# A decoder layer on one core: row buffers turned by one slot, two weight pieces behind the first queries, and another order of VectorE's steps in the first attention turn

## What is computed

```python
x = x + s5(layernorm(x))        # scan over axis 0 (4 steps): z = Re-pair of V(A z + u), u = Vinv dt x; 2*Re(z)
x = x + xattn(layernorm(x), ctx) # 16 heads of 32, softmax over the sequence's 77 context rows, Wq Wk Wv Wo
x = x + ffn(layernorm(x))        # W_exp (512->2048), butterfly of 11 stages, gelu,
                                 # butterfly of 11 stages, W_con (2048->512), biases
return x                         # all float32
```

## Time and profile before

| | us |
|---|---|
| median of 3 runs | 2254.57 (2254.3 to 2255.26) |
| the profiled execution | 2254.27 |
| its span, first to last instruction | 2252.1 |
| stage one, up to the first scores | 253.6 |

### The profile page before, as it was taken

One profiled execution on the slowest core, in us unless ns is written; L12 is line 12 of the kernel. 1 busy time (PEld: TensorE's weight loads), 2 busy tenths in 40 slices (PEclk: granted clock), 3 DMA queues, 4 the chain that ended last, 5 costly groups with the idle time before them and its releaser, 6 DMA issues.

```text
span 2252.1 us, 41275 instructions
## 1 busy us (share of the span) xinstructions
PE 2215.3 (98%) x15960; PEld 1938.7 (86%) x15960; DVE 1701.0 (76%) x2854; ACT 1229.4 (55%) x2735; POOL 466.2 (21%) x578
## 2 busy tenths in 40 slices
PE   8999889999999999999999999999999999999999
PEld 7788678888888888789989989989989989889899
DVE  6775688888888888867957858758669678579467
ACT  3666566766666776635535436446346355355343
POOL 3530222222322223200110300300300300300203
PEclk8999899999999999999999999999999999999999
DMA  8999623323323331476686786786686776766765
GB/s 319 338 353 312 204 94 109 109 83 122 124 86 113 108 106 62 162 259 187 215 264 178 223 266 177 222 267 203 194 268 208 220 233 212 245 206 213 226 189 194
DMA packets 202091, 443.35 MB, mean 197 GB/s; under 512 B 32442, under 2 KB 70586, under 8 KB 200362
## 3 DMA queue, kind: packets, MB, share of 16 engines
q1 hardware_dynamic: 201898, 440.72, 60.5%
HBM read 341.66 MB, written 99.01 MB: 196 GB/s over the span
## 4 chain that ended last, share of the span: by engine, by line
PE 84%; DVE 6%; ACT 5%; DMA 3%; issue 1%; SPq 0%; POOL 0%; DVEq 0%; ACTq 0%; POOLq 0%
PE ps L455 68%; PE ps L2005 5%; PE ps L1973 4%; PE ps L1984 2%; ACT es L1099 2%; DMA x_scratch<-xa 2%; PE ps L1937 1%; ACT wc_h L1055 1%; PE ps L1894 1%; PE ps L1825 1%; DVE st L1292 1%; DVE rsum L1507 1%; ACT es L1104 1%; DMA x<-x_scratch 1%; DVE ql L1329 1%
## 5 line engine op out<-in xcount | busy, mean ns | idle before, releaser
L455 PE MATMUL ps<-ring,gh 128*128 128x256 f32 x3584 | 652.8, 284 | 0.1
L455 PEld LDWEIGHTS ps<-ring,gh 128*128 128x128 f32 x3584 | 558.3, 192 | 2.1 <-DVE gl L1329 1.5
L455 PE MATMUL ps<-xth,ring 128*128 128x512 f32 x1792 | 553.4, 389 | 0.6 <-ACT U L1209 0.6
L455 PE MATMUL ps<-ring,gl 128*128 128x256 f32 x1792 | 506.9, 283 | 0.0
L455 PEld LDWEIGHTS ps<-xth,ring 128*128 128x128 f32 x1792 | 336.4, 188 | 70.7 <-issue 1.0
L1197 ACT ACTIVATE gh<-G 128x512 fp32r<-128x512 f32 x384 | 239.2, 629 | 218.7 <-PE ps L455 218.3
L455 PE MATMUL ps<-xtl,ring 128*128 128x512 f32 x896 | 348.6, 389 | 0.0
L455 PEld LDWEIGHTS ps<-ring,gl 128*128 128x128 f32 x1792 | 343.5, 192 | 0.0
L1329 DVE TENSOR_TENSOR gl<-G,gh 128x512 fp32r<-128x512 f32 x384 | 276.1, 731 | 51.3 <-ACT gh L1197 50.2
L1180 ACT ACTIVATE G<-G,up_b 128x512 f32<-128x512 f32 x192 | 138.9, 723 | 222.0 <-DVE G L1625 222.0
L880 POOL TENSOR_TENSOR es<-es,rinv 128x308 f32<-128x308 f32 x256 | 180.0, 735 | 386.3 <-DVE rinv L1511 386.3
(11 more groups left out here) (234 smaller groups left out, 4379.3 us busy)
## 6 DMA issues: line engine op xcount, KB each, us to landing
ring<-wup_scratch SPq DMA_DIRECT2D x224, 512.0 KB, 3.8
ring<-wdn_scratch SPq DMA_DIRECT2D x224, 512.0 KB, 3.7
X<-x_scratch SPq DMA_DIRECT2D x32, 1024.0 KB, 8.8
xa<-in_x SPq DMA_DIRECT2D x16, 1024.0 KB, 8.8
x_scratch<-xa SPq DMA_DIRECT2D x16, 1024.0 KB, 10.8
x<-x_scratch SPq DMA_DIRECT2D x16, 1024.0 KB, 5.6
x_scratch<-x SPq DMA_DIRECT2D x16, 1024.0 KB, 4.3
out_x<-X SPq DMA_DIRECT2D x15, 1024.0 KB, 7.8
```

The lines of the kernel that those rows point to most:

```text
L455: mm = pe.matmul(bank, a, b, start=first and i == 0, stop=last and i == n - 1, skip_group_check=go_on)
```

## The change

The ring of row buffers is turned by one slot: group `g` uses `(g + 4) % 5`, so group 15 uses slot 4, and slots 0 to 3 come free one group earlier. `x1[0]`, `x1[1]` and `x1[2]` are loaded in groups 12, 13 and 14; `x1[2]`'s load after stage one goes. Slot 4 is now under `qh` (written from the second group's first query on, which gets a wait for all sixteen stores), and `wqh` goes where `qh` was; its copy waits for piece 56 instead of the store of group 11. `X` and `rawx` of the FFN move by 8 KB to match. Group 15 has three pieces; the last two, 70 and 71, go on PE behind the first four queries, on ScalarE behind the four high copies of them, on SyncE behind the store of group 15. PE's wait for all pieces moves behind scores(0) of the first turn. In that turn VectorE makes `lo_p(0, 0)` ahead of `shift(2)`, `lo_p(1, 0)` ahead of `shift(3)` and `lo_q(3)` ahead of the mixing of the first FFN weights; its waits for the stage buffers and the cleared buffer move up with `lo_p(0, 0)`.

```diff
-    wqh = r2.put("wqh", [P, KC, D], F32R)
+    qh = r2.put("qh", [P, KC, GT], F32R)
...
-    qh = r2.put("qh", [P, KC, GT], F32R)
+    wqh = r2.put("wqh", [P, KC, D], F32R)
...
-    r3 = Region(free_first)
+    r3 = Region(free_first + 4 * KC * GT)
...
-        PER_GROUP = [0, 0, 6, 6, 5, 5, 5, 5, 5, 5, 5, 5, 5, 5, 5, 5]
+        PER_GROUP = [0, 0, 6, 6, 5, 5, 5, 5, 5, 5, 5, 5, 5, 5, 5, 3]
+        LATE = range(PIECES - 2, PIECES)
-        xslot = lambda g: (g + 3) % XS
+        xslot = lambda g: (g + 4) % XS
...
-                        n = g - (NG - 3)
-                        if n in (0, 1):
+                        n = g - (NG - 4)
+                        if n in (0, 1, 2):
                             after(sp, x1_loaded, n * 16)
...
+            for n in LATE:
+                piece_out(n)
             stored(sp, x1_stored, NG - 1)
-            load_x1(2)
...
-                        act.wait_ge(x1_stored, 16 * (NG - 4))
+                        act.wait_ge(piece_pe, DL)
...
+            for n in LATE:
+                piece_back(n)
...
                     exp(2)
+                    act.wait_ge(x1_stored, 16 * NG)
                     hi_q(0)
...
                     sums(1)
-                    shift(2)
                     for i, out in enumerate(stage_out):
                         dve.wait_ge(out, stage_turns(PIECES, i))
                     dve.wait_ge(p_zero, 1)
                     lo_p(0, 0)
+                    shift(2)
                     lo_q(0)
                     spread2(2, range(0, 2))
                     lo_q(1)
                     sums(2)
+                    lo_p(1, 0)
                     shift(3)
-                    lo_p(1, 0)
                     spread2(2, range(2, T))
                     sums(3)
                     lo_q(2)
+                    lo_q(3)
                     mix_weights(0)
-                    lo_q(3)
...
             for o in range(KC):
                 query(ps[:, o, :], o).then_inc(pre_pe, 1)
+            for n in LATE:
+                piece(n)
             pe.wait_ge(x1_ready, KC * NG)
-            pe.wait_ge(piece_act, PIECES)
...
                 if g == 0:
                     scores(0)
+                    pe.wait_ge(piece_act, PIECES)
```

More of the change, by code:

```diff
@@ L243, in decoder_layer @@
     spots = []
-    for at, end in ((after_keep, after_keep + 4 * T * D), (r3.at, es_end)):
+    for at, end in ((after_keep, after_keep + 4 * T * D), (free_first, free_first + 4 * KC * GT), (r3.at, es_end)):
         while at + 4 * 2 * GT <= end:
@@ L463, in decoder_layer @@
         PIECES = 4 * MC + 8
-        PER_GROUP = [0, 0, 6, 6, 5, 5, 5, 5, 5, 5, 5, 5, 5, 5, 5, 5]
-        assert sum(PER_GROUP) == PIECES and len(PER_GROUP) == NG
+        PER_GROUP = [0, 0, 6, 6, 5, 5, 5, 5, 5, 5, 5, 5, 5, 5, 5, 3]
+        LATE = range(PIECES - 2, PIECES)
+        assert sum(PER_GROUP) + len(LATE) == PIECES and len(PER_GROUP) == NG
         VALUES_AT = (0, 2), (1, 0), (1, 2)
         stage_turns = lambda n, i: 16 * ((n - i + STAGES - 1) // STAGES)
-        xslot = lambda g: (g + 3) % XS
+        xslot = lambda g: (g + 4) % XS
         x_turns = lambda g: 16 * (g // XS + 1)
```

## The result

| | before | after |
|---|---|---|
| median of 12 runs each | 2255.07 us (2249.69 to 2257.01) | 2258.83 us (2255.39 to 2262.46) |
| the profiled execution | 2254.27 us | 2257.13 us |
| its span | 2252.1 us | 2254.9 us |

The ratio is 1.0021 [1.0013, 1.003]: slower by a hair over 0.2%, some 4.7 us; the two medians themselves lie 3.8 us apart. The forecast was 2256.7 us, and the median lies 2.1 us above it; against the kernel before it was +2.4 us, where 3.8 to 4.7 were measured.

The account below looks back on a forecast made before the run. TensorE is busy 98% of the span, so only some 11 us of idleness and 4 us of slow clock could be touched. +3.8 us at the third maxima less 1.4 gave 2254.3 + 2.4 = 2256.7 us, range 2250.3 to 2260.5.

Parts of the forecast that it names:

- the gate: First turn: GpSimd's clearing waits for the late stores, so the first transposes of probabilities start at 267.7 us, 3.8 later.
- my own signs: Prediction wrong if clearing starts before 260 us, group 12's store lands at 215.4, or 292 us's shift isn't the end's.
- The slip of group 12's store: SyncE's queue: the earlier first row load puts 1 MB ahead of this store, making it 2.6 us later; bounds 0 and 3.5.
- The transposes of the normalised rows: PE, before the first queries: they wait for ScalarE behind piece 68's copy and start at 234.6 us, against 235.07.
- neither gain nor loss: At the first scores: 0.5 us and the shorter group set against a longer stretch at half clock, taken as zero.
- rival (a): Slip absent or late stores not last; the load taken off the path gives nothing: 2254.1 us, chance 0.22.
- the late stores landing with group 15's: SyncE's stores of the two late pieces land where group 15's store landed, 260.48 plus the slip: 263.1 us.
- rival (b): Group 14's store lands 4.5 us earlier, slip small, clock holds, queries start 5 us earlier: 2249 us, chance 0.14.
- rival (c): PE idles some 4 us ahead of the first transposes of probabilities, the clock falls, +2.6 us: 2259.3 us, chance 0.20.
- VectorE's order: First turn, third maxima to next turn's first maxima: 23.04 - 2.0 + 0.6 = 21.6 us, a gain of 1.4 us.
- now run while PE makes the third scores: First turn: three low copies of 0.68 us on VectorE leave the stretch behind the third maxima, -2.0 us.
- From there on each turn follows the one before: After the next turn's maxima: the shift of +2.4 us there goes unchanged to the end.

Follow-up runs that it names:

- kernel 1: The changed kernel measured again with no edit, against the kernel before: 2259.36 us, ratio 1.0022.
- kernel 3: The changed kernel with `wqh` put between `xt2l` and `kh`, 16384 bytes from `xt2h`: 2255.52 us, ratio 1.0009 to the kernel before.
- kernel 7: The changed kernel with 128 bytes ahead of `wqh`, making its distance to `xt2h` 21504 bytes: 2258.8 us, one execution.
- kernel 8: kernel 3 with 384 bytes ahead of `wql` and all buffers behind it, distance of `wqh` to `xt2h` still 16384: 2257.35 us, one execution.
- kernel 6: kernel 3 with GpSimd's wait for the stage buffers and clearing of `pt2` moved behind the first tile's multiplications: 2252.27 us, ratio 0.9988 to the kernel before.
- kernel 10: The changed kernel, placement kept, with GpSimd's clearing moved behind the first multiplications: 2255.58 us, ratio 1.001 to the kernel before.
- kernel 11: kernel 6 measured again beside kernel 9 and kernel 10 on one chip: 2252.16 us, ratio 0.9991 to the kernel before.
- kernel 4: The kernel before with only VectorE's new order in the first attention turn: 2252.74 us, ratio 0.9992.
- kernel 2: The kernel before with only `wqh` and `qh` exchanged, FFN buffers moved by 8 KB and the copy's wait changed: 2257.35 us, ratio 1.0019.
- kernel 9: kernel 4 with GpSimd's clearing moved behind the first multiplications: 2253.49 us, ratio 0.9991 to the kernel before.

## Why the prediction was right or wrong

The time came out inside the range and near the forecast, and that is in part luck: a loss of 3.6 us that I hadn't in my sum, 14 turns of slower query matmuls, stands where the sum had the gate. By my own signs the account was wrong in two of three points for the first profile: the clearing started at 257.97 us and not after 260, and the shift of -1.20 us at 290 us wasn't the shift at the end, +2.87. In kernel 1, where the clearing came at 260.27 us, the shift still grew, from +0.47 to +4.62.

**The slip of group 12's store: right in kind, too large.** 216.94 less 215.39 is 1.55 us, not 2.6, in the first profile; the size of single landings varies as much as that.

**The transposes of the normalised rows: right in place.** 233.92 us where I had 234.6, by the smaller slip; ScalarE's copy of piece 68 (230.45 us) stands ahead of them, as worked out. But I took neither gain nor loss from there to the first scores, and the first maxima came 1.18 us earlier, no more than such shifts vary between kernels with the same code up to there. At the medians nothing is left: with the ring and without late pieces the ratio is 0.9994, and the order alone has 0.9992. The 3 us that VectorE no longer waits for the load are worth nothing measurable, as rival (a) said of this edit.

**The gate: right, with a landing put together wrongly.** I had the late stores landing with group 15's, at 263.1 us. They land 3 to 4 us behind it: in the first profile group 15's store ahead of 254.41, when the loads of values begin, and the late pieces just ahead of 257.97. What made up for it was group 14's store, out of rival (b): held until 248.06 us instead of 251.45. So the clearing came at 257.97. In four of the five profiles with late pieces and the clearing in its old place it came at 258.3 to 261.4 us, PE waited 1.3 to 3.9 us for GpSimd, and the clock was low: kernels 1, 3, 7 and 8 lost 3.2, 5.9, 7.3 and 6.1 us in the first turn, kernels 6, 10 and 11, with the clearing moved, 0.5, 0.6 and 0.8. In these four the third maxima came 4.3 to 7.0 us later against the first ones, 1.55 us of it by the moved low copies (kernel 4); I had 3.8, and 6.4 with rival (c), whose low clock, to which I gave 0.20, goes with the gate in each of the four. I held it off because the idleness would be shorter than 3.43 us; in kernel 1 the clock was low from 258 us already, ahead of the wait, and stayed low through a wait of 1.32 us. How much of the loss is the wait and how much the clock isn't told apart. Nor did earliness help: in kernel 3 all was 4.5 us early, the clearing (258.34 us) but little, and PE stood 3.92 us. The late pieces landing behind the store that was issued ahead of them is in line with the ring's order that the Trainium skill states ("DMA: Bandwidth & Descriptors", "Queues, rings and completion order").

**VectorE's order: the stretch right, the term wrong.** The waits came where I put them, 2.18 and 0.51 us against 2.2 and 0.4, and the next transposes took over the wait of the moved copy (1.15 us). The stretch shrank by 2.05 us, where I had 1.4. But the sentence that the three copies "now run while PE makes the third scores" fails: in kernel 4 the scores cover half a microsecond of them, and the third maxima come 1.55 us later. Net -0.5 in the profile; by medians 0.9992 [0.9983, 1.0002], not clear of no gain. I counted the first copies as free because I measured from the maxima behind them.

**"From there on each turn follows the one before": failed.** This is the step that decides. "The moved buffers keep their sizes" was all that I said of them, and the exchange is worth +3.6 us in the profiles, 1.0019 at the medians: as much as the largest term of my sum, the 3.8 us of the gate, and put at nothing. Nothing in the trace of before could have priced it, but bounding it from both sides was what the change called for. Without it, the change is at 1.0009 [0.9996, 1.0021] with the gate and at 0.9988 to 0.9991 without.

**Still open.** The runs of the changed kernel fall into two groups, six of 2255.4 to 2257.1 us and six of 2260.5 to 2262.5. I took the gate for the cause; but kernel 2, which has no late pieces, scatters alike (six runs of 2254.6 to 2255.9, five of 2260.5 to 2264.1, one of 2258.8). The changed kernel's second set doesn't part in two: its eleven runs lie between 2252.6 and 2263.6 us without such a hole, and its profiled execution, with the gate, took 2258.8 us, in the hole of the first set. Whether there are two groups at all, and what would part them, isn't shown. How much the gate costs at the median is known only across chips: 1.0021 and 1.0022 against 1.001, and 1.0009 against 0.9988 and 0.9991, some 2.5 to 4.7 us, with intervals that overlap or all but touch. What shows the gate's cost are the profiles: 3.2 to 7.3 us in the first turn with it, 0.5 to 0.8 with the clearing moved.

## What to carry to other kernels

A buffer that an inner loop reads is not moved for free: compare the mean time of its matmuls in a stretch that nobody edited, and look where the shift between two traces grows, not only how large it is at the end. Where an engine waits for a DMA's landing and the work behind that wait doesn't need it, put the work first; such a wait is harmless until some other edit makes the landing two microseconds later. When instructions move ahead of a mark, measure from a mark ahead of them both.

## What the runs showed of the hardware

With identical matmuls the step from one to the next was 227 ns on average where `wqh` and `xt2h` lie 24576, 16384 or 21504 bytes apart in a partition (all multiples of 512), and 232 to 235 ns at 21376 bytes. The third form, whose `wql` and `xt2h` were not moved in the change, slowed as well (390 to 397 ns), so it isn't simply each matmul's own pair; the distance from `wqh` to `wql`, which changed by the same amount, isn't ruled out as the cause. Whether 256, 512 or 1024 bytes is the unit isn't told apart (the three quick distances are multiples of all of them, 21376 of none), and other distances weren't tried.

The landing of one megabyte scatters. SyncE's queue behind the store of group 14, in kernel 4 and then in kernel 9, whose code is the same up to there:

```profile
233.46 16.08 SPq L560 DMA_DIRECT2D wd_scratch<-stage  x5
```

```profile
234.36 11.97 SPq L560 DMA_DIRECT2D wd_scratch<-stage  x5
```

Four microseconds lie between the two. A step of a sum that rests on one such landing can be off by as much.
